# A convolutional attention kernel on one core: the first maximum tile of a pair of heads moved into the fourth projection tile, the others one place on

## The reference, cut to what matters

```python
xn = _group_norm(xf, gamma, beta)                              # 512 x 1024
qkv = jnp.einsum('oc,bcl->bol', w_qkv, xn) + b_qkv[None, :, None]
q, k, v = jnp.split(qkv, 3, axis=1)                            # 8 heads of 64 channels
weight = jnp.einsum('bct,bcs->bts', q * scale, k * scale)      # 1024 x 1024 a head
weight = jax.nn.softmax(weight.astype(jnp.float32), axis=-1)
a = jnp.einsum('bts,bcs->bct', weight, v)
hid = jnp.einsum('oc,bcl->bol', w_proj, hid) + b_proj[None, :, None]
return (xf + hid)
```

## Time and profile before

| | |
|---|---|
| median of 3 runs | 2454.15 us (2452.81 to 2454.8) |
| the profiled execution | 2451.95 us |
| its span, first to last instruction | 2450.3 us |
| mean granted TensorE clock | 0.996 of full speed |
| busy: TensorE, VectorE, ScalarE, GpSimd | 2417.2, 1602.5, 1165.6, 1184.9 us |
| chain that ended last | 94% TensorE |

### The profile page before, as it was taken

One profiled execution on the slowest core, in us unless ns is written; L12 is line 12 of the kernel. 1 busy time (PEld: TensorE's weight loads), 2 busy tenths in 40 slices (PEclk: granted clock), 3 DMA queues, 4 the chain that ended last, 5 costly groups with the idle time before them and its releaser, 6 DMA issues.

```text
span 2450.3 us, 37583 instructions
## 1 busy us (share of the span) xinstructions
PE 2417.2 (99%) x12980; PEld 1610.7 (66%) x12980; DVE 1602.5 (65%) x2100; ACT 1165.6 (48%) x1563; POOL 1184.9 (48%) x590
## 2 busy tenths in 40 slices
PE   8999999999899999999999999999999999999999
PEld 7888888888655575557556655755575566557555
DVE  6554554555667756775677577567756765775677
ACT  4332333323355645654555456356545554562554
POOL 3330000000066755773766667467737665571674
PEclk9999999999899999999999999999999999999999
DMA  6332111013221251205122322512151233212021
GB/s 189 134 112 73 51 68 68 34 45 127 78 95 48 100 188 61 104 28 214 35 101 99 136 79 75 198 44 104 52 189 35 112 112 113 104 44 104 35 69 44
DMA packets 73977, 226.75 MB, mean 93 GB/s; under 512 B 12288, under 2 KB 12288, under 8 KB 72960
## 3 DMA queue, kind: packets, MB, share of 16 engines
q1 hardware_dynamic: 59296, 172.01, 19.8%
q0 software_dynamic: 14560, 52.96, 6.0%
HBM read 141.05 MB, written 71.30 MB: 87 GB/s over the span
## 4 chain that ended last, share of the span: by engine, by line
PE 94%; POOL 2%; DVE 2%; issue 1%; ACT 1%; DMA 0%; ACTq 0%; SPq 0%; POOLq 0%; DVEq 0%
PE psum L1617 18%; PE psum L1598 14%; PE psum L1557 14%; PE psum L1370 11%; PE psum L1389 7%; PE psum L1738 7%; PE psum L1568 7%; PE psum L1413 4%; PE psum L1441 4%; POOL a_all L613 2%; PE psum L1636 2%; PE psum L1487 2%; PE psum L1381 1%; PE psum L1657 1%; PE psum L1501 1%
## 5 line engine op out<-in xcount | busy, mean ns | idle before, releaser
L613 POOL TENSOR_TENSOR a_all<-a_all 128x1024 f32<-128x1024 f32 x410 | 1010.2, 2464 | 498.5 <-ACT a_all L852 463.4
L852 ACT ACTIVATE a_all<-psum 128x1024 f32<-128x1024 f32 x512 | 496.3, 1022 | 81.7 <-PE psum L1598 69.1
L1152 DVE TENSOR_REDUCE small<-psum 128x2 f32<-128x1024 f32 x326 | 399.0, 1226 | 167.6 <-PE psum L1568 167.6
L1617 PE MATMUL psum<-a_all 128*64 128x512 f32 x2048 | 495.7, 605 | 0.0
L1598 PE MATMUL psum<-r_all 64*128 64x512 f32 x3200 | 415.6, 392 | 3.4 <-ACT a_all L852 2.0
L1557 PE MATMUL psum<-r_all 128*128 128x512 f32 x1536 | 364.6, 396 | 4.5 <-DVE r_all L1269 4.5
L1598 PEld LDWEIGHTS psum<-r_all 64*128 64x128 f32 x3200 | 300.2, 185 | 72.6 <-ACT a_all L852 13.8
L1557 PEld LDWEIGHTS psum<-r_all 128*128 128x128 f32 x1536 | 286.2, 189 | 84.9 <-issue 23.3
L1617 PEld LDWEIGHTS psum<-a_all 128*64 128x64 f32 x2048 | 124.0, 136 | 233.0 <-issue 172.6
L1370 PE MATMUL psum<-r_all 128*128 128x512 f32 x1152 | 271.7, 394 | 2.3 <-DVE r_all L1019 2.3
L1370 PEld LDWEIGHTS psum<-r_all 128*128 128x128 f32 x1152 | 215.2, 189 | 58.3 <-DVE small L1152 5.7
(11 more groups left out here) (157 smaller groups left out, 2628.0 us busy)
## 6 DMA issues: line engine op xcount, KB each, us to landing
r_all<-w_dram SPq DMA_DIRECT2D x48, 1024.0 KB, 5.0
xn_dram<-a_all POOLq DMA_DIRECT2D x56, 512.0 KB, 6.7
r_all<-xn_dram SPq DMA_DIRECT2D x7, 4096.0 KB, 15.3
a_all<-x SPq DMA_DIRECT2D x16, 1024.0 KB, 7.0
y_dram<-a_all SPq DMA_DIRECT2D x16, 1024.0 KB, 4.2
a_all<-y_dram SPq DMA_DIRECT2D x8, 2048.0 KB, 10.7
out<-a_all SPq DMA_DIRECT2D x28, 512.0 KB, 4.0
a_all<-sums SPq DMA_DIRECT2D x192, 64.0 KB, 2.0
```

The source lines that it names most:

```text
L613: pool.tensor_tensor(to, probs[:, 0, :, cols] if i == 1 else to, probs[:, i % SLOTS, :, cols], ALU.add).then_inc(sum_step, 1)
L852: act.activation(probs[:, i % SLOTS, :, cols], psum[half][:, :, :], ACT.Exp, scale=SCALE).then_inc(probs_ready, 1)
L1152: dve.reduce_max(max2[:, :, tile, half], of[:, :, :], AX_X).then_inc(work_free, 2)
L1617: last = pe.matmul(psum[2][h * D:(h + 1) * D, half], v_t[:, i, head], probs[:, i % SLOTS, h, half * HALF:(half + 1) * HALF], start=(i == 0 ...
```

## The change

Maximum 0 of a pair now stands in the middle of projection tile 3, behind 6 of its 12 matmuls; maximum 1 follows behind tile 3, and each later one stands where the one before it stood. So weigh 6 and weigh 7 follow each other with no maximum between them. To make `psum[3]` free in time, query half 0 is projected to `psum[1]` and half 1 stays in `psum[2]`. `COPIED` becomes 4 to 14. On VectorE `q_lo` of the two query halves follows maxima 0 and 1, the two `hid_lo` follow maximum 2, and the reciprocals follow maxima 3, 5, 7, 9. The last pair of the last batch has no next pair and stays as it was.

```diff
         def q_bank(half):
-            return psum[3 - half][:, half]
+            return psum[1 + half][:, half]
...
-        COPIED = tuple(range(3, MAXES - 2, 2))
+        COPIED = tuple(range(4, MAXES - 1, 2))
...
-                        if more and 2 * i - 1 in COPIED:
-                            copy_max(pairs, 2 * i - 1)
+                        if more and 2 * i in COPIED:
+                            copy_max(pairs, 2 * i)
...
                     next_qk(1)
-                    next_qk(2)
-                    if p >= 2:
-                        for h in range(NH):
-                            hid_lo(b, p - 2, h)
+
+                    def late_hid():
+                        if p >= 2:
+                            for h in range(NH):
+                                hid_lo(b, p - 2, h)
+
+                    if not more:
+                        late_hid()
...
-                            if m == 0:
-                                next_qk(3)
-                            if p and m in (2, 4, 6, 8):
+                            if m < 2:
+                                next_qk(2 + m)
+                            if m == 2:
+                                late_hid()
+                            if p and m in (3, 5, 7, 9):
                                 invert_sums(b, p - 1, m // 2 - 1, 1)
...
-            def qk_tile(slot, i, before=lambda j: None):
+            def qk_tile(slot, i, before=lambda j: None, between=None):
...
                 for j in range(CT):
                     before(j)
+                    if between and j == CT // 2:
+                        between()
...
+                    if i == 0 and half == 1 and more:
+
+                        pe.wait_ge(q_free[0], pairs + 2)
...
-                            if i == 2:
-
-                                pe.wait_ge(work_free, work.upto())
-                            qk_tile(p % 2, i)
+                            qk_tile(p % 2, i, between=next_max if i == QK - 1 else None)
...
                                 pe.wait_ge(qk_hi_done, (pairs + 2) * QK - 1)
-                                pe.wait_ge(q_free[0], pairs + 2)
-                            if m == 1:
+                            if m == NT // 2:
...
                             weigh(b, p, i - 1, more)
-                            next_max()
+                            if i < NT - 1:
+                                next_max()
                     weigh(b, p, NT - 1, more)
```

More of the change, by code:

```diff
@@ L1729, in batch1 @@
                             weigh(b, p, i - 1, more)
-                            next_max()
+                            if i < NT - 1:
+                                next_max()
                     weigh(b, p, NT - 1, more)
-                    assert made[0] == MAXES
+                    assert made[0] == MAXES or not more
                 def proj_steps(to, o, half, js):
```

## The result

The changed kernel takes 2475.42 us, the median of 4 runs (2470.91 to 2476.31), against 2454.28 us for the kernel before (2452.81 to 2454.8): a ratio of 1.0084, with a 95% interval of 1.0072 to 1.0097. It is slower, as forecast, by 21 us where 15 were forecast; the median lies 0.4 us above the upper end of the range. The profiled execution has a span of 2473.7 us, 23.4 more than before; the prediction's sum for it had said 15.7. (The profiled execution of the kernel before, 2451.95 us, is 0.9 us faster than the fastest of the runs above; hence 23.4 here and 21 there.)

A forecast was written before the change was run, and what follows sets the result against it. The prediction took TensorE's chain, busy for 99% of the span, as the bound. Its terms, 1.6 + 2.4 + 6.9 + 0.7 + 4.1 = +15.7 us, gave 2467.7 us profiled and a median near 2469, range 2456 to 2475.

The forecast's parts named there:

- cut less join, 31 pairs: Cutting tile 3 costs 0.62 us, joining weigh 6 and 7 gains 0.57: +0.05 us a pair, +1.6 us in all.
- hid_lo in the loop, 12 pairs: In loop batches hid_lo starts 0.16 us before GpSimd's addition and delays maximum 4: 0.2 us a pair, +2.4 us.
- hid_lo in the written-out batches, 3: GpSimd starts 0.02 us ahead there and holds hid_lo off, delaying maximum 4: 2.3 us in three pairs, +6.9 us.
- maximum 1 of the fourth pair, 6: GpSimd's lateness makes VectorE late at maximum 0 of the next fourth pair: 6 x 0.12 = +0.7 us.
- sums at a batch's end: The sums wait there for GpSimd's last addition, 0.82 us later against TensorE, less 0.13 slack: six times, +4.1 us.
- The rule of mode changes: On TensorE, a tiling mode change drains the array; two removed and two added, so cut and join give about nothing.
- GpSimd first everywhere: Rival: GpSimd starts before hid_lo in all 15 pairs, 2.3 us each, 36 us slower, 2490 us; 10%.
- no conflict: Rival: hid_lo has no port conflict with GpSimd, so only 6.3 us slower, 2460.5 us; 20%.
- The rule of the Trainium skill cited in the prediction: VectorE operations with two SBUF inputs contend with GpSimd's SBUF reads; whoever issues first has the port for the whole instruction.
- GpSimd's lateness, met again: GpSimd's later end returns at the next fourth pair, +0.7 us, and at six batch ends, +4.1 us.
- The release of the banks: Two maxima need 1.90 us; maximum 0 to 1 will be 2.0, so no wait if VectorE is free.
- likeliest case: hid_lo starts first in the loop, GpSimd first in the written-out batches; near 2469 us, own range 2466 to 2473; 35%.

The follow-up runs named there:

- experiment 5: Kernel before with the cut alone: maximum 0 inside projection tile 3, no join, hid_lo where they were; 2463.99 us, ratio 1.0041.
- experiment 3: Kernel before with only the two hid_lo moved, behind maximum 1; no cut, no join; 2465.08 us, ratio 1.0046.
- experiment 1: Changed kernel with the two hid_lo one maximum earlier, behind maximum 1 instead of 2; 2463.15 us, ratio 1.0037 to the kernel before.
- experiment 8: Changed kernel with maximum 2 ahead of the sums, hid_lo still behind it; 2459.8 us, ratio 1.0024 to the kernel before.
- experiment 7: Changed kernel with the two hid_lo one maximum later, behind maximum 3; 2546.0 us, ratio 1.0377 to the kernel before.
- experiment 6: Changed kernel with GpSimd's last addition of the fourth pair left out in batches 1 to 7; 2469.36 us, ratio 1.0068 to the kernel before.
- experiment 4: Kernel before with maximum 1 moved ahead of the sums in 23 pairs; 2452.31 us, ratio 0.9994.
- experiment 2: Changed kernel with GpSimd's first addition waiting for both hid_lo in third and fourth pairs; 2475.48 us, ratio 1.0086 to the kernel before.

## Why the prediction was right, and where it was short

The profiled execution lost 23.4 us; its steps, with what the distances and rows of the two profiles give for each:

```
step                                      forecast    measured
cut less join, 31 pairs                      1.6       2.5   (31 x 0.08)
hid_lo in the loop, 12 pairs                 2.4       1.8   (12 x 0.15)
hid_lo in the written-out batches, 3         6.9       7.0   (2.28 + 2.28 + 2.40)
maximum 1 of the fourth pair, 6              0.7       1.1   (6 x 0.18)
sums at a batch's end                        4.1       3.9   (6 x 0.72 less 0.45)
sum of the steps                            15.7      16.3
half clock behind two of the long waits       -        3.1   (1.5 + 1.6)
VectorE late in the written-out batches       -        0.9   (0.27 + 0.51 + 0.55 less 0.4)
scores of a second pair                       -        0.7   (about 0.1 each)
ahead of the first turn, and the end          -        1.7
not placed                                    -        0.7
```

- **Bound.** Right: TensorE's own work hardly changed, and the loss is in its waits.
- **Cut and join.** Right that they cancel; +0.08 us a pair, with the joined weighings at 3.58 us (1678.39 to 1681.97) in place of 4.16. The cut is 0.65 where 0.62 was forecast (experiment 5). The rule of mode changes that the prediction took from the Trainium skill (TensorEngine Tiling (Array Packing), section Key Properties) fits: as many changes as before, and nearly the same time.
- **`hid_lo` and GpSimd.** Shown, from both sides. It costs near 9 of the 11 us that experiment 3 loses without cut and join; it goes away when the `hid_lo` are earlier (1) or GpSimd's start later against them (8); it strikes all 15 pairs when they are later (7). Which of the two comes first decides: `hid_lo` is 0.15 to 0.17 us ahead in the loop, 0.01 to 0.03 behind in the written-out batches, in three separately built kernels (the changed one, 3 and 6). The rival "GpSimd first everywhere" is what experiment 7 makes, the rival "no conflict" what experiments 1 and 8 make. The rule of the Trainium skill cited in the prediction (SBUF — State Buffer, section Who interferes with whom) is borne out by these rows for `hid_lo` too: 0.74 us becomes 2.89, and in the loop 2.37 becomes 2.80.
- **GpSimd's lateness, met again.** Right in kind and size: 0.72 us at a batch's end where 0.69 was forecast, shown by experiment 6, which takes it away. At the end of the seventh batch it is a gain: there the sums stood 6.13 us behind before, 5.68 now, since TensorE itself is late by two long waits. The sum had left this end out.
- **The release of the banks.** 2.02 us from maximum 0 to maximum 1, as forecast, in the loop's second and third pairs. In three pairs of the written-out batches it is 2.29, 2.53 and 2.57, which the sum had not (0.4 us of it is no loss, since the kernel before has maximum 0 late by 0.10 to 0.16 in the same pairs). The reduction of maximum 0 starts 1.26 us after it there (2374.25, 2375.51) and not 0.62, because VectorE's pair begins late. The rows are those of the eighth batch's third pair, and last the `end_add` of the fifth batch's third pair.

```profile
2367.57 1.23 DVE L1240 TENSOR_TENSOR a_all<-a_all 128x1024 f32<-128x1024 f32 x1 [5.20 <-POOL a_all L613]
...
2375.51 1.22 DVE L1152 TENSOR_REDUCE small<-psum 128x2 f32<-128x1024 f32 x1
...
2374.25 0.50 PE L1576 MATMUL psum<-u,r_all 64*128 64x512 f32 x2
...
2376.78 0.50 PE L1576 MATMUL psum<-u,r_all 64*128 64x512 f32 x2 [0.43 <-DVE small L1152]
```

```profile
1684.47 1.23 DVE L1240 TENSOR_TENSOR a_all<-a_all 128x1024 f32<-128x1024 f32 x1 [4.35 <-POOL a_all L613]
```

  Against the pair's turn (2367.20 and 1684.84), `end_add`, which GpSimd releases, starts 0.37 us behind in the one and 0.37 ahead in the other. All pairs but the one with VectorE's stall fit this: with `end_add` 0.3 us or more ahead of the turn maximum 1 comes at 2.02 or 2.03; at +0.04 (every fourth pair of the loop) at 2.20, at +0.24 at 2.29, at +0.37 at 2.53, at +0.51 at 2.57. So this is GpSimd's lateness once more, as far as rows can tell; no run tests it by itself. That GpSimd ends later against TensorE in the written-out batches holds for the kernel before as well (`end_add` 0.1 to 0.3 ahead of the turn there, 0.8 to 1.0 in the loop); why was not tested.

- **What was short.** The steps held; the sum lacked terms that follow from them. A wait of 2.2 us on TensorE was priced at 2.2. In two of three places TensorE's clock halved behind it, for 1.5 and 1.6 us more: these two stretches take 91.34 and 46.22 us from turn to turn, and 89.87 and 44.63 in experiment 6, which has the same waits and no half clock behind them. Experiment 3 has none behind them either. That it comes and goes fits the runs of the changed kernel: the one at 2470.91 us has a mean clock of 0.997, those at 2475.24 to 2476.31 have 0.994 or 0.995. What makes the clock fall in one case and not in the other was not tested. The measured time also lies above the likeliest case's own range (2466 to 2473), though its mechanism is the one that came. Without the 3.1 us of half clock it would lie inside the stated range, as the run of 2470.91 us does.
- **Slips in the prediction.** 2467.7 and 2.2 are 2469.9, not 2469. Two times 7.31 us and the 15.72 of six additions differ by 1.1, not 1.0. The gain at the seventh batch's end and VectorE's lateness in the written-out batches were left out.
- **Open.** The 1.1 us ahead of the first turn is found in every rebuilt kernel (turns at 692.7 to 694.2, before 692.13) and wasn't traced. It speaks against the change as its cause that experiment 4, without cut, join or moved `hid_lo`, has it too (693.31), and that the profiled execution of the kernel before lies 2.3 us below that kernel's median; but this is not shown.

## What to carry to other kernels

When an operation moves on an engine, ask what the neighbouring engine runs at the new place, and not only whether the engine itself is idle there: the two `hid_lo` lengthened nothing where they stood, and cost near 9 us of the kernel when they were moved to where GpSimd starts within 0.2 us of them. A gain on the bounding engine is kept only as far as its partners get it too; here a join worth 0.57 us a pair turned into a wait at each batch's end, because GpSimd's additions had 0.18 us of slack. And where a long wait is forecast on TensorE, allow for the clock behind it.

## What the hardware showed beside this

- Two starts 0.02 us apart settle 2.1 us of VectorE's time, the same way each time: all nine pairs of the written-out batches in the changed kernel and in experiments 3 and 6, with their 0.01 to 0.03 us, went to GpSimd, which was ahead.
- The loser paid what the winner had left, less 0.15 to 0.19 us, whichever engine it was. A `hid_lo` with 2.34 us of GpSimd's addition before it took 2.15 longer (2.89 for 0.74); GpSimd with 0.58 us of a `hid_lo` before it took 0.43 longer (2.80 for 2.37); the first `hid_lo` of experiment 7, with 1.29 us of an addition left, took 1.10 longer (1.84 for 0.74).
- The granted clock of 0.50 appears in the profile of every kernel here, the one before too, in stretches near 50 us, at 640 to 655 us and at its end; in between it is found behind long waits alone: behind two of the nine waits of 2.2 to 2.3 us for a `hid_lo` (the changed kernel, experiments 3 and 6), behind twelve of the fifteen longer ones of experiment 7, and behind VectorE's stall in experiments 1, 2, 3, 6, 7 and 8, but not in the kernel before, the changed one, 4 and 5. One such stretch costs a profile 1.4 to 1.6 us.
